# Unread identity products on TensorE ahead of two waits in an eight-image fused network kernel

## The reference

```python
x = x + _L0_conv_ref(_gn(x), ...)      # linear attention behind a 5x5 depthwise convolution
x = x + _L1_conv_ref(_gn(x), ...)      # 3x3 convolution with signed weights
t = _to_tokens(x)                      # 256 tokens of 64 channels an image
t = t + _L2_attn_ref(_ln_t(t), ...)    # 16 heads: causal, selected and window attention
t = t + _L2_ffn_ref(_ln_t(t), ...)     # mixture of 8 experts, two per token
t = t + _L3_attn_ref(_ln_t(t), ...)    # linear attention, 8 heads
t = t + _L3_ffn_ref(_ln_t(t), ...)     # 8 experts, routed by image
x = _from_tokens(t, x)

def _gn(v, G=32, eps=1e-05):           # group norm ahead of the first two stages
    g = v.reshape(B_, G, C_ // G, H_, W_)
    m = jnp.mean(g, axis=(2, 3, 4), keepdims=True)
    s = jnp.var(g, axis=(2, 3, 4), keepdims=True)
    return ((g - m) / jnp.sqrt(s + eps)).reshape(v.shape)

def _ln_t(v, eps=1e-05):               # layer norm of each token
    m = jnp.mean(v, axis=-1, keepdims=True)
    s = jnp.var(v, axis=-1, keepdims=True)
    return (v - m) / jnp.sqrt(s + eps)
```

## Time and profile before

| | us |
|---|---|
| median of 3 runs | 995.24 (992.84 to 999.41) |
| the profiled execution, its own time | 998.67 |
| its span, first to last instruction | 996.6 |
| PE busy | 877.7 (88% of the span) |
| PE weight loads busy | 585.3 (59%) |
| DVE busy | 595.7 (60%) |
| ACT busy | 457.9 (46%) |
| POOL busy | 204.8 (21%) |
| mean granted TensorE clock | 0.943 of full speed |

### The profile page before, as it was taken

How to read it: one execution, slowest core, us unless ns; L and a number is a source line. 1 busy time by engine, 2 the same in 40 slices (tenths; PEclk the granted TensorE clock), 3 DMA queues, 4 the chain that set the end, 5 groups by cost and what they waited for, 6 DMA issues and landing times.

```text
span 996.6 us, 22072 instructions
## 1 busy us (share of the span) xinstructions
PE 877.7 (88%) x9104; PEld 585.3 (59%) x9104; DVE 595.7 (60%) x1666; ACT 457.9 (46%) x764; POOL 204.8 (21%) x274
## 2 busy tenths in 40 slices
PE   9887898989999899988998898899998888878877
PEld 8675565546666655665666565565655555544553
DVE  4545535672688368845883588447864764553456
ACT  1003336453545355535562554346446554524754
POOL 1002101120133022501240134112411241130122
PEclk9999699999999999999999999799999999887988
DMA  7100000000000000000000000000001000030000
GB/s 196 24 7 1 1 6 22 23 28 22 23 22 23 28 22 23 22 28 22 22 23 28 22 23 23 22 1 22 23 28 38 22 22 23 22 80 22 2 1 22
DMA packets 25572, 25.82 MB, mean 26 GB/s; under 512 B 14689, under 2 KB 20577, under 8 KB 25345
## 3 DMA queue, kind: packets, MB, share of 16 engines
q1 hardware_dynamic: 25472, 24.42, 8.5%
HBM read 19.69 MB, written 4.72 MB: 24 GB/s over the span
## 4 chain that ended last, share of the span: by engine, by line
PE 56%; DVE 19%; ACT 11%; issue 6%; DMA 4%; POOL 2%; SPq 1%; POOLq 0%; DVEq 0%; ACTq 0%
PE ring L930 7%; PE side_a L630 6%; PE pv L969 5%; ACT pr L1186 4%; PE pv L951 4%; PE ring L885 4%; DVE rden L1672 4%; PE side_a L639 2%; DMA scale<-branch_scale 2%; PE heads L875 2%; PE heads L910 2%; PE ring L893 2%; DMA branch_scale<-rden 2%; DVE img L1391 2%; PE ring L925 2%
## 5 line engine op out<-in xcount | busy, mean ns | idle before, releaser
L1186 ACT ACTIVATE pr<-ring 128x1024 f32<-128x1024 f32 (+1 forms) x128 | 120.9, 944 | 112.5 <-PE ring L934 62.4
L930 PE MATMUL ring<-kq 64*128 64x256 f32 (+2 forms) x1280 | 137.8, 344 | 0.7 <-ACT kq L1238 0.5
L930 PEld LDWEIGHTS ring<-kq 64*128 64x128 f32 x1280 | 97.4, 193 | 43.0 <-issue 31.1
L1682 DVE SCALAR_TENSOR_TENSOR ob<-pv,all_gates,scale 128x256 f32<-128x256 f32 x96 | 46.3, 482 | 88.2 <-PE pv L969 44.7
L1657 DVE TENSOR_REDUCE toks<-heads 128x2 f32<-128x512 f32 x64 | 44.3, 692 | 90.7 <-PE heads L915 89.3
L1230 ACT ACTIVATE kq<-ring 128x896 f32<-128x896 f32 x64 | 58.8, 919 | 83.2 <-PE ring L885 83.2
L573 POOL TENSOR_TENSOR toks<-ta,tb 128x128 f32<-128x128 f32 (+1 forms) x96 | 39.8, 434 | 186.7 <-DVE tb L1648 186.7
L1238 ACT ACTIVATE kq<-ring 128x256 f32<-128x256 f32 x64 | 24.6, 384 | 116.4 <-PE ring L893 115.9
L536 POOL TENSOR_TENSOR oT<-ob 128x256 f32<-128x256 f32 x32 | 23.3, 728 | 233.2 <-DVE ob L1682 233.2
L1672 DVE RECIPROCAL rden<-pv 128x256 f32<-128x256 f32 x32 | 56.2, 1756 | 24.7 <-PE pv L951 24.2
L885 PE MATMUL ring<-early,toks 128*128 128x128 f32 x448 | 63.4, 283 | 7.8 <-ACT pr L1186 7.8
(11 more groups left out here) (375 smaller groups left out, 1691.1 us busy)
## 6 DMA issues: line engine op xcount, KB each, us to landing
scale<-branch_scale SPq DMA_DIRECT2D x128, 96.0 KB, 2.3
branch_scale<-rden SPq DMA_DIRECT2D x32, 128.0 KB, 1.7
late<-in_late SPq DMA_DIRECT2D x1, 2158.5 KB, 8.4
xin<-in_x SPq DMA_DIRECT2D x16, 64.0 KB, 2.2
pr<-in_prep SPq DMA_DIRECT2D x1, 602.0 KB, 3.8
y<-ob SPq DMA_DIRECT2D x8, 64.0 KB, 1.9
kq<-in_masks SPq DMA_DIRECT2D x1, 480.0 KB, 8.5
toks<-in_final SPq DMA_DIRECT2D x1, 434.0 KB, 4.3
```

The costliest lines, as they stand in the source:

```text
L930: m = pe.matmul(ring[:, j, at:at + nq], kq[rows, k, key0:key0 + P], kq[rows, k, Q + q_:Q + q_ + nq], start=r % 2 == 0, stop=at > P)
L1186: act.activation(out, in_, ACT.Exp, scale=SCALE).then_inc(S("exp_done"), 1)
L1682: V.scalar_tensor_tensor(out=ob[:, g % 2, br, :], in0=PV[:, 0:T], scalar=all_gates[:, of, br:br + 1], in1=scale[:, br, :], op0=ALU.mult, o ...
```

## The change

Four lines of PE's program. In `front`, for the third to the eighth image, PE now waits for `gn1_var` and then runs four identity products into `SA`, before its wait for `gn1_done`. In `back`, for all eight images (there is no condition on the image here), four identity products into `SB_` stand between the output projection's step and the wait for `xn2`.

```diff
@@ front, TensorE
                 yield
                 busy_until(n, "gn1_done")
+                if n > 2:
+                    after(n, "gn1_var")
+                    busy(4, SA)
                 after(n, "gn1_done")
                 if n == 1:
                     pe.wait_ge(S("conv_weights"), 5)
@@ back, TensorE
                 m.then_inc(S("attn_out"), 1)
                 yield
+                busy(4, SB_)
                 after(n, "xn2")
                 transpose_tok(xp, SB_, 0, "xn2_turned")
                 yield
```

## The result

The changed kernel takes 987.49 us (median of 11 runs, 977.51 to 990.11) against 997.82 us for the kernel before, measured beside it (11 runs, 991.92 to 999.41). The ratio is 0.9891, with a 95% interval from 0.9863 to 0.9919: 1.1% faster, about 10 us. The forecast was 979. The execution that was profiled took 981.87 us, the second fastest of the eleven; before, the profiled one took 998.67.

What follows compares the result with a forecast made beforehand. The prediction took PE to set the pace: 998.67 us less 6.6 (convolutions) and 9.4 (turnings) gives 982.7, less 3.9 for even odds on the long low run gives 978.8, said as 979; range 966 to 990.

Steps and rivals of the forecast that it cites:

- What the drops are and what four products cost: Slow clock makes convolutions 7.6 not 5.93 us, turnings 6.32 not 4.75; four products cost 0.98 us at the high level.
- The sum of 16.0 us: Convolutions give 6.6 us and turnings 9.4, taking the profiled 998.67 us to 982.7.
- the ten drops that were counted: Low-clock stretches at the convolutions of images 4 to 7 and the turnings of images 1 to 5 and 7.
- the range named this: The main case's own range, 967 to 986, allowed that low slices at the clock line's end can ease too.
- the two terms: 6.6 us from the products ahead of the convolution, 9.4 us from those ahead of the turning.
- the turnings keep theirs, because of the thin work: Rival: thin work around the turning causes its drop, so only convolutions gain 6.6 us; 992, chance 0.06.
- The drops only move: Rival: remaining waits such as L786 take over, the number of low stretches stays; 997 to 999, chance 0.07.
- Even odds: 3.9 us less: The long low run near 622, behind L786's idle, costs 7.8 us and may go as that idle shifts in time.
- a long low run in every image: Rival: L786's idle brings the 7.8 us in each image behind the fourth, five times; 1014, chance 0.05.
- convolutions or turnings that keep their drops: Within the main case's own range, one or two drops that stay, 1.6 us each; as whole rivals 989 (0.09) and 992 (0.06).
- two gaps without a drop that the prediction calls just as long: Idle of 2.44 us ahead of image 8's convolution and 1.01 us at image 6's turning, both with the clock staying high.

Runs made afterwards that it cites:

- fifth experiment: Kernel before plus eight identity products right behind the convolution's first group in images 3 to 8, where PE does not wait; 1007.28 us against 999.98, ratio 1.0061.
- in the second: Changed kernel measured once more against the kernel before: 988.67 us against 999.98, ratio 0.9873; its profiled execution took 991.41 us.
- more waits filled: Changed kernel with m3 waits filled, plus eight products each ahead of kv3_normed (images 7, 8) and xn4 (image 8); 977.55 us against the kernel before's 999.98.

## Why the prediction was right, and where it was off

**What the drops are and what four products cost: right.** The convolutions went from 7.6 to 5.93 us, the turnings' follow-up from 6.32 to 4.75, and four products cost 0.96 us where nothing hides them (0.98 was the price). The added wait for `gn1_var` held nothing: the products of image 4 start at 223.25, behind the scores as foreseen. The interval between convolutions fell to 99.63 us in the first of them, 99.4 was named; the next two are 101.37, with no low stretch in it, and 102.22, with the one near 512.

**The sum of 16.0 us: right for the pair of profiled executions, in part by luck.** 998.67 - 981.87 is 16.8 us, and the ten drops that were counted are gone. But two amounts that the sum left out cancel. Behind 857 us the clock was low for 33.5 us before and is for 23.9 now, which is worth about 5 us; the range named this, the sum did not. And about as much went to waits that were not there before, as in the interval of 101.37 us: the low stretches shrank by 44 us in all, which is worth 22, and the time by 16.8. The pair is also a lucky one: the profiled execution of the changed kernel is 5.6 us below its median, the one before 0.9 us above its own.

**That the two terms belong to the two edits: wrong, as far as the turnings go.** The prediction took 9.4 us as the worth of the turnings' products. But with the convolution's products alone the turnings' drops vanished as well, twice, behind an unfilled wait of 1.15 us. Either edit alone reached 0.986 to 0.990, as much as both together (0.987 to 0.989). So 6.6 and 9.4 are not two gains to be added: a removed drop moves everything behind it, and waits that had a drop can be without one. The fifth experiment shows this with work that fills no wait. The rival "the turnings keep theirs, because of the thin work" was not borne out anywhere. "The drops only move" holds in a small part: those at `m3` came back at other images, but between 200 and 850 us the clock was low for 47.8 us before and is for 17.1 now.

**"Even odds: 3.9 us less" for the long low run: this is the term that came out wrong.** The prediction took the run near 622 for a matter of alignment that might go. It is tied to one wait, `m3`, and in the changed kernel it is there in other images instead: once long and once short in the first profiled execution, three times in the second. The drops at `m3` cost 8.5 us before (13.7 and 3.4 us at the low level) and the same 8.5 in the first, so the term was 0 there and not 3.9, and about 3 us worse than 0 in the second. Here the forecast and the measurement part: the median is 987.5 and not 979, which is still in the range, near its upper end, though the range had reckoned there with convolutions or turnings that keep their drops. With the `m3` wait filled the median is 979.0, and the low slices of the middle are gone. The rival "a long low run in every image" named the right place, but the run came in at most three images and its whole price was 12 us, where the rival added 31.

**Why that wait is there** is read from the trace: `m3` stands in DVE's queue behind the weighing L1686, which waits for a DMA. A faster PE does not shorten that DMA, and the wait of PE grew from 1.23 us to 1.60 us in the fifth image. That the DMA is the cause of the differences from one execution to the next is argued, not shown.

**What stays open.** The idle time alone does not decide: 1.60 us dropped the clock, 1.35 us ahead of the convolution did not, 2.14 us at the sixth image's `m3` of the same execution did not, and 0.36 us at `m3` in the next one did. There the products around are thin (one column, or bf16 of 48 rows), but no run took thin work alone away.

The Trainium skill's page TensorE: Matmul & The Clock Gate asks in the section "Why this matters for your kernels", against drops in the middle of a kernel, only that long idle gaps be avoided. By that rule this change would have brought nothing. The runs decide otherwise: filling gaps of 2.4 and 1.2 us brought 10 us, and the `m3` gap 8.5 more. (Of the two gaps without a drop that the prediction calls just as long, only image 8's 2.44 us is; image 6's is 1.01 us where 1.16 us had one.)

## What to carry to other kernels

Where the granted clock falls for a few microseconds behind short waits, unread matmuls in those waits are nearly free and can pay back 1.6 us a drop. But count drops over several executions and not in one profile: each removed drop moves the rest, so single gains do not add up. Here what remained stood at the next unfilled wait. Fill the whole set of such waits before judging one of them: the third place brought 8.5 us on top of the first two, nothing on top of one of them, and alone no more than the noise allows.

## What the runs showed of the hardware that was not expected

Adding about 11 us of PE work in places without idle made the kernel only 7.3 us slower (2 to 10 by the interval), and took the drops away from a wait that was left as it was. One low run lasts about 14 us though PE is then busy without a break (12.00 of 12.00 us in the stretch from 716 to 728): once low, the clock does not always come back at once while this kernel's attention work runs, while the drops at the convolutions were over within its 7.6 us in all cases but one (8.91 us in the fifth experiment). And the spread of the run times narrows as waits are filled: 12.6 us in the changed kernel, 4.8 with `m3` filled, 2.9 with more waits filled. That the low runs set it is argued and not shown.
